# Normalised value sums of a half team: taken by VectorE out of PSUM, without ScalarE's copy to SBUF

## What is computed

```python
qkv = (x @ W_qkv.T).reshape(b, n, 16, 8).transpose(0, 2, 1, 3)      # one matrix for q, k and v
score = softmax(einsum('bhif,bhjf->bhij', qkv, qkv) / sqrt(8), axis=-1)
attn = einsum('bhij,bhjf->bihf', score, qkv)
out = attn.reshape(b, n, 128) @ W_o.T
...
x = x + 0.5 * ffn(layernorm(x));  x = x + attention(layernorm(x));  x = x + 0.5 * ffn(layernorm(x))
```

## Time and profile before

| | |
|---|---|
| median of 3 runs | 1315.32 us (1313.44 to 1316.38) |
| the profiled execution's own time | 1316.4 us |
| its span in the trace | 1314.7 us |
| granted TensorE clock, mean | 0.975 |
| attention in the trace | about 385 to 1075 us |

### The profile page before, as it was taken

The page is one execution under the profiler, slowest core; times in us unless marked ns, Lnnn a source line. Parts: engine busy times, 40 slices in busy tenths (PEclk is TensorE's granted clock), DMA queues, the critical chain, the costliest instruction groups (busy, mean ns, idle before and its releaser), DMA issues.

```text
span 1314.7 us, 27184 instructions
## 1 busy us (share of the span) xinstructions
PE 1157.7 (88%) x9031; PEld 635.2 (48%) x9031; DVE 1135.0 (86%) x2367; ACT 889.2 (68%) x1879; POOL 470.5 (36%) x515
## 2 busy tenths in 40 slices
PE   3847999888599999999999999999998889999993
PEld 2746888777123333333323233233322258778882
DVE  7877888887899999989998999999999468988885
ACT  1224555555178999898888888888887965555651
POOL 3873547343113001314225313333333117643222
PEclk9999999999589999999999999999999999999997
DMA  8125565554010200002001000001000403554653
GB/s 275 52 70 184 204 208 188 218 214 130 28 34 19 66 15 6 18 20 64 2 28 37 12 28 18 18 27 27 18 5 22 176 33 120 207 195 178 255 201 138
DMA packets 58616, 123.54 MB, mean 94 GB/s; under 512 B 12352, under 2 KB 33826, under 8 KB 58448
## 3 DMA queue, kind: packets, MB, share of 16 engines
q1 hardware_dynamic: 49488, 103.83, 23.0%
q0 software_dynamic: 8704, 16.93, 4.1%
q10 hardware_dynamic: 288, 1.05, 0.2%
HBM read 36.66 MB, written 23.88 MB: 46 GB/s over the span
## 4 chain that ended last, share of the span: by engine, by line
PE 51%; DVE 29%; POOL 6%; issue 5%; ACT 4%; DMA 4%; SPq 1%; DVEq 0%; POOLq 0%; ACTq 0%
DVE att_neg_part L1959 15%; PE psum L2267 12%; PE psum L2181 7%; PE psum L2245 7%; PE psum L2169 7%; PE psum L2171 6%; PE psum L2228 4%; POOL rows_dram L1252 4%; DVE att_neg_part L1964 3%; DMA ffn_block_rows<-rows_dram 2%; DVE stats L1593 2%; DVE ffn_x2c L1900 2%; ACT att_probs L1445 1%; DVE ffn_hidden L1911 1%; PE psum L2121 1%
## 5 line engine op out<-in xcount | busy, mean ns | idle before, releaser
L1445 ACT ACTIVATE att_probs<-psum 128x512 f32<-128x512 f32 x1024 | 555.4, 599 | 59.3 <-PE psum L2249 30.8
L1959 DVE TENSOR_REDUCE att_neg_part<-psum 128x2 f32<-128x1024 f32 x443 | 520.2, 1217 | 32.2 <-PE psum L2229 30.4
L2267 PE MATMUL psum<-att_probs,att_values 128*16 128x256 f32 x4096 | 322.4, 387 | 12.4 <-ACT att_o_t L1460 7.7
L1413 ACT ACTIVATE ffn_silu<-ffn_x2c,ffn_rec 128x256 f32<-128x256 f32 (+1 forms) x320 | 154.7, 487 | 169.3 <-DVE ffn_x2c L1900 168.1
L1268 POOL DMA_INDIRECT y_dram<-ffn_y,ffn_block_rows x144 | 142.4, 989 | 234.5 <-ACT ffn_y L1431 206.3
L2249 PE MATMUL psum<-att_right,att_left 64*128 64x512 f16 x512 | 199.7, 390 | 18.8 <-DVE att_neg_part L1959 13.2
L2228 PE MATMUL psum<-att_right,att_left 62*128 62x512 f16 x512 | 199.3, 390 | 16.3 <-DVE att_neg_part L1959 11.7
L2245 PE MATMUL psum<-att_right,att_left 64*128 64x512 f16 x512 | 199.6, 390 | 8.1 <-DVE att_neg_part L1959 6.7
L2229 PE MATMUL psum<-att_right,att_left 62*128 62x512 f16 x512 | 200.9, 393 | 0.0
L1900 DVE TENSOR_SCALAR ffn_x2c<-psum,ffn_rec 128x256 f32<-128x256 f32 (+1 forms) x320 | 162.6, 512 | 35.9 <-PE psum L2171 31.8
L2169 PE MATMUL psum<-ffn_block_t,ffn_rec 128*128 128x256 f32 (+1 forms) x640 | 178.6, 361 | 1.2 <-ACT ffn_block_t L1364 1.2
(11 more groups left out here) (236 smaller groups left out, 1171.6 us busy)
## 6 DMA issues: line engine op xcount, KB each, us to landing
ffn_rec<-record SPq DMA_DIRECT2D x80, 776.5 KB, 3.8
ffn_block_rows<-rows_dram SPq DMA_DIRECT2D x64, 130.0 KB, 3.1
record<-in_L_ffn_W SPq DMA_DIRECT2D x16, 256.0 KB, 6.5
att_left<-q_parts_dram SPq DMA_DIRECT2D x64, 64.0 KB, 2.2
y_dram<-ffn_y,ffn_block_rows POOLq DMA_INDIRECT x144
x_sb<-in_L_attn_x SPq DMA_DIRECT2D x4, 512.0 KB, 7.1
record<-in_L_ffn_Wo SPq DMA_DIRECT2D x8, 256.0 KB, 7.0
rows_dram<-rows,place_i POOLq DMA_INDIRECT x128, 2.4
```

The lines of the kernel that those rows point to most:

```text
L1445: S.activation(probs[:, slot % PROBS, :], ring_bank(("score", slot))[:, :], ACT.Exp, scale=unlift).then_inc(att_bank.by_act, 1)
L1959: last = V.tensor_reduce(out=neg_part[:, h % 2, keys, p::PAIR, t], in_=psum[:, low:high + 1, :], axis=AX.X, op=ALU.max, negate=True)
L2267: last = TE.matmul(value_bank[head * VS:head * VS + VW, q], values[:, b % 2, kt, team * TEAM + head, :], probs[:, (UNIT * n + j) % PROBS, ...
```

## The change

ScalarE's part of step 1 is left out for the 31 half teams whose transposes lie in the ring. VectorE's reciprocal and product read the bank of the transposes. The bank is released by VectorE's product (semaphore `finished`, in the trace `team_half_finished`), and the counts of `bank_emptied` leave those banks out. The last half team keeps its copy.

```diff
     def emptied(self, name):
         size, n = self.number[name]
-        return (self.by_act if size == 1 else self.reduced), n
+        if size == 2:
+            return self.reduced, n
+        if name in self.read_by_dve:
+            return self.by_dve, self.read_by_dve[name]
+        return self.by_act, self.emptied_by_act(n)
...
                 if at == step and part[0] == 0:
-                    att_bank.plan(name)
+                    att_bank.plan(name, by_dve=2 * which[0] + which[1] + 1 if what == "finish" else 0)
...
-            elif what == "finish" and step == 1:
+            elif what == "finish" and step == 1 and which == (NTEAM - 1, 1):
                 side = banks_of(("finish", which))
                 S.wait_ge(*side.full(("finish", which)))
                 S.copy(o_t[:, which[1], :], ring_bank(("finish", which))[:, :]).then_inc(side.by_act, 1)
...
             elif what == "finish" and step == 2:
-                o = o_t[:, half, :].rearrange("p (t j d) -> p t j d", t=HT, j=TEAM)
-                V.wait_ge(*banks_of(("finish", which)).emptied(("finish", which)))
+                if which == (NTEAM - 1, 1):
+                    o = o_t[:, half, :].rearrange("p (t j d) -> p t j d", t=HT, j=TEAM)
+                    V.wait_ge(*side_bank.emptied(("finish", which)))
+                else:
+                    o = ring_bank(("finish", which)).rearrange("p (t j d) -> p t j d", t=HT, j=TEAM)
+                    V.wait_ge(*att_bank.full(("finish", which)))
                 settle(V.reciprocal(inv_sum[:, :, :], o[:, :, :, DH]))
...
                 TE.wait_ge(reduced, MAX_UNITS)
-                TE.wait_ge(att_bank.by_act, att_bank.count[1])
+                TE.wait_ge(att_bank.by_act, att_bank.emptied_by_act(att_bank.count[1]))
+                TE.wait_ge(finished, 2 * NTEAM - 1)
```

More of the change, by code:

```diff
@@ L55, with __init__, plan @@
 class Ring:
-    def __init__(self, banks, filled, by_act, maxed, reduced):
+    def __init__(self, banks, filled, by_act, maxed, reduced, by_dve):
         self.banks = banks
-        self.filled, self.by_act, self.maxed, self.reduced = filled, by_act, maxed, reduced
+        self.filled, self.by_act, self.maxed, self.reduced, self.by_dve = filled, by_act, maxed, reduced, by_dve
         self.at, self.number, self.holders = {}, {}, []
         self.count = {1: 0, 2: 0}
-    def plan(self, name, size=1):
+        self.read_by_dve = {}
+    def plan(self, name, size=1, by_dve=0):
         assert name not in self.at, name
@@ L71, in plan, with emptied_by_act @@
         self.number[name] = (size, self.count[size])
+        if by_dve:
+            self.read_by_dve[name] = by_dve
+    def emptied_by_act(self, n):
+        return n - sum(self.number[name][1] <= n for name in self.read_by_dve)
     def bank(self, name, k=0):
@@ L450, in build_macaron @@
                       for b in range(B)]
-        att_bank = Ring(7, semaphore("bank_full"), semaphore("bank_emptied"), maxed, reduced)
+        att_bank = Ring(7, semaphore("bank_full"), semaphore("bank_emptied"), maxed, reduced, finished)
         side_bank = Banks([value_bank], semaphore("side_full"), semaphore("side_emptied"))
```

## The result

The changed kernel takes **1343.87 us** (median of 6 runs, 1340.95 to 1345.22), the kernel before on the same chip 1314.20 (6 runs, 1313.44 to 1316.38): a ratio of **1.0221** (of the means), 95% interval 1.0208 to 1.0234; the medians differ by 29.7 us. The profiled pair differs by 27.3 us (1343.68 against 1316.4) and in its spans by 26.7, so the traces hold nearly all of it. The forecast was 1336, within 1320 to 1348.

A forecast was written before the change was run, and what follows sets the result against it. VectorE was taken to pace the attention, idle 0.47 of 19.45 us in a plain half team. Terms of -1.5, +16.5, +3.0 and +2.2 sum to +20.2 us on the 1315.3 us median: forecast 1336 us, range 1320 to 1348.

The forecast's parts named there:

- rival A: Bank of the transposes held too long, VectorE waits for TensorE once per half team: 1325 to 1345 us, chance 0.72.
- The round trip: At each finish, round 10's row maximum waits for VectorE's product: 0.55 us in 28 half teams, +16.5 us in all.
- TensorE's lateness: In about ten half teams with extra TensorE work, part of its 1.07 us delay shows: 0.3 us each, +3.0 us.
- PSUM reads: 31 reciprocals and 31 products of VectorE read PSUM instead of SBUF: +2.2 us, within 0 and 4.0.
- ScalarE's relief: 31 copies leave ScalarE's queue: 1 us gained through earlier value-sum copies, 0.5 us at the attention's end, -1.5 us.
- B: Same wait, but relieved ScalarE brings TensorE forward before round 8's reduction, 0.55 shrinks to 0.15 us: 1322 us, chance 0.14.
- C: ScalarE is the pacer, each half team gains its copy's 0.48 us: 14.9 us less, 1300 us, chance 0.07.
- D: TensorE is the pacer everywhere, its whole 1.07 us counts in 30 half teams: +34 us, 1349 us, chance 0.07.

The follow-up runs named there:

- The kernel with only the hold: Kernel before, ScalarE's copy and SBUF reads kept; only the transposes' bank is held until VectorE's product: 1342.85 us, ratio 1.0197.
- the two orders that let the bank go in time: Changed kernel with VectorE's reciprocal and product one round earlier (1310.10 us, ratio 0.9958), or with TensorE's transposes one round later (1326.77 us, ratio 0.9968, another chip).

## Why the prediction was right, and where it was not

**The forecast's mechanism held** (rival A). The kernel with only the hold has the whole loss in the attention (25.7 of 25.8 us), and the two orders that let the bank go in time have none of it.

**Step by step.**

- *The round trip, 28 x 0.55 + 0.27 + 0.79 = +16.5.* Measured: the reduction starts 0.57 us later against the product's end than before in 28 half teams (in one of them, with TensorE at the lower clock, 0.79). At the two odd finishes the gap is 0.71 (0.44 before) and 0.70 (none), so 0.27 and 0.78 with the overlap of the rows. 28 x 0.57 + 0.27 + 0.78 = 17.0. The 0.55 was worked out from two rows of the kernel before, 0.05 and 0.42, and both are found in the kernel after.
- *TensorE's lateness, +3.0.* This is the step that failed, in size and place. I put it in ten half teams, those with output rows or preparation, with 0.3 us each. Of the 25.8 us in the attention, 8.8 are left beside the round trip. The output-row half teams have nothing of it (0.59 us, as the plain ones). It sits where VectorE's own chores delay the product: TensorE waits there not for the 0.94 us of a plain half team but for 2.0, and in most such cases its clock fell for 3.4 us. I had taken 1.07 us as the most that TensorE could lose at a finish, from the plain half team alone. Moving the value products ahead of the wait took back 9.5 us (707.8 to 698.3), about this amount.
- *PSUM reads, +2.2 within 0 and 4.0.* Measured +0.2. The nearest rows disagreed (2 and 65 ns), and I gave the reciprocal the dearer one because it reads one tensor; the runs show 5 ns. The Trainium skill, page "VectorE: DVE Perf Modes", section on the TRN2 errata, gives an estimate of 4.0; this case's trace does not agree for these two shapes.
- *ScalarE's relief, -1.5 within 0 and -6.7.* The copy cut to half gave 0.0% (-0.13 to +0.15%), and the kernel with only the hold differs from the changed one by 0.1 us in the attention. So its value is about 0, within some 2 us. Work off an engine that is waiting turned into more waiting: ScalarE's idle time ahead of the exponentials rose from 59.3 to 89.1 us by the hold alone, and to 110.4 with the copies gone as well.

So the forecast's sum of 20.2 us becomes 26.0 with the terms as measured: +0.5 on the round trip, +5.8 on TensorE's lateness, +1.5 for a relief that was none, -2.0 on the PSUM reads. The attention shows 25.8; that the two agree proves nothing, since the 8.8 was taken as what is left, and its independent support is the 9.5 of the reordered kernel. The profiled pair differs by 27.3, the medians by 29.7; the 1.5 us outside the attention and the 2.4 between pair and medians belong to no step of mine. That the time lies within my range is partly luck. With every term at the dear end that I gave it (PSUM 4.0, ten half teams at 0.52, no relief) the sum was 1341 us, and the measured 1343.87 is beyond it; A's end of 1345 takes up to 1.07 for the ten, which counts their 0.55 a second time, and comes to 1346.

**The rivals.** B, largely paid back, is excluded: the old gap of 0.42 us is still ahead of round 8's reduction, and the new one is beside it. C is excluded by the result itself, which is slower, and by the half-size copy. D, the full 1.07 us everywhere, would have made a plain half team 20.5 us; it was 20.1. Its total, 1349, lies only 5 us above the measured one, though TensorE does not set the plain half teams' pace: the lost 8.8 us came in single half teams instead.

**What stays open.** Twelve of the 14 waits of 2.0 us (seven in the changed kernel, seven in the one with only the hold) were followed by the lower clock, two were not, and no run says why. The 7.2 us above are what the half teams with such a stretch lost, not what a run with the clock alone changed has shown; the comparisons above give 0.5 to 1.5 us for one.

## What to carry to other kernels

When a buffer's reader is changed from one engine to another, the cost is in the ring: count the places to the next user of the buffer, and ask whether the new releaser, at its own place in its own order, is then in time. If it is not, and what it wants next comes out of that buffer, each turn costs a full round trip (here 0.57 us) on the engine that sets the pace, and here the 16 us of work saved on another engine covered none of it. The direct read was worth having here only after producer and reader had been put in the same round, and then it was 0.3 to 0.4% faster than before.

## What the hardware showed that I had not expected

- TensorE's granted clock fell from 1.00 to 0.50 (2.4 to 1.2 GHz) for about 3.4 us at 12 of 14 waits of 1.99 to 2.07 us, starting between 0.1 us before and 1.7 us behind the end of the wait; never so close behind the same wait where it was 0.94 to 1.23 us, nor behind one of 1.44 to 1.51 where the value products had been put ahead. A matmul of 128x512 took 0.63 us there instead of 0.39. So a wait of one engine, hidden in the plain half teams, cost more where it was twice as long.
- VectorE took at most 5 ns longer from PSUM than from SBUF in these two shapes: 248 against 243 ns for a reciprocal of 128x16, 291 against 291 for a product of 128x128.
